# Sparse graph attention layer: roots of the second phase's layer norms by Newton steps on VectorE in place of ScalarE

## The reference

```python
def _ln(x, g, b):
    mu = jnp.mean(x, axis=-1, keepdims=True)
    var = jnp.var(x, axis=-1, keepdims=True)
    return (x - mu) * jax.lax.rsqrt(var + EPS) * g + b
...
z = _ln(x, ln1_g, ln1_b)
q, k, v = z @ Wq + bq, z @ Wk + bk, z @ Wv + bv       # per head
scores = jnp.einsum('ehd,ehd->eh', q[row], k[col]) * scale + bias
alpha = softmax of scores over the edges of each row
att = segment_sum(alpha * v[col], row) @ Wo + bo
x1 = x + att
z = _ln(x1, ln2_g, ln2_b)
ff = jax.nn.silu(z @ W1 + b1) @ W2 + b2
return _layernorm(x + (x1 + ff))
```

## Time and profile before

| | |
|---|---|
| median of 3 runs | 4988.64 us |
| lowest and highest run | 4966.76 and 5004.79 us |
| profiled execution: span | 4610.2 us |
| profiled execution: its own time | not given beside the span |
| TensorE busy, matmul | 3227.0 us (70%) |
| VectorE busy | 2862.0 us (62%), 6445 instructions |
| ScalarE busy | 2094.3 us (45%), 6748 instructions |
| GpSimd busy | 3100.7 us (67%), 3033 instructions |
| chain that ended last, by engine | issue 23%, PE 21%, POOL 16%, DVE 14%, DMA 11%, DVEq 9%, ACT 3% |
| mean granted TensorE clock | 0.794 |

### The profile page before, as it was taken

One profiled execution on the slowest core, in us unless ns is written; L12 is line 12 of the kernel. 1 busy time (PEld: TensorE's weight loads), 2 busy tenths in 40 slices (PEclk: granted clock), 3 DMA queues, 4 the chain that ended last, 5 costly groups with the idle time before them and its releaser, 6 DMA issues.

```text
span 4610.2 us, 73226 instructions
## 1 busy us (share of the span) xinstructions
PE 3227.0 (70%) x18717; PEld 2461.0 (53%) x18717; DVE 2862.0 (62%) x6445; ACT 2094.3 (45%) x6748; POOL 3100.7 (67%) x3033
## 2 busy tenths in 40 slices
PE   4576877776877546777677776777777777777766
PEld 3344444444444235666565665656656555656655
DVE  9766666666666335666556665666565565665654
ACT  0011112111111135666566666666566566665664
POOL 0177777777777767777777777777676676666752
PEclk5577766777767668888888888888888888888888
DMA  4233333333334355655666656665665665656542
GB/s 168 66 113 115 107 102 112 109 102 107 112 100 111 102 192 188 208 183 184 222 203 214 214 196 205 221 214 182 213 210 166 210 206 190 203 185 211 189 150 82
DMA packets 282999, 756.58 MB, mean 164 GB/s; under 512 B 92435, under 2 KB 94675, under 8 KB 281862
## 3 DMA queue, kind: packets, MB, share of 16 engines
q0 software_dynamic: 213664, 577.32, 38.1%
q1 hardware_dynamic: 68454, 169.70, 12.1%
HBM read 759.20 MB, written 58.87 MB: 177 GB/s over the span
## 4 chain that ended last, share of the span: by engine, by line
issue 23%; PE 21%; POOL 16%; DVE 14%; DMA 11%; DVEq 9%; ACT 3%; POOLq 1%; ACTq 1%; SPq 0%; PEld 0%; PEldq 0%
POOL records L378 8%; PE bank L1144 7%; DMA records<-rec_w,pos_i 5%; PE bank L1179 5%; POOL region_a L447 5%; DVE region_c L864 4%; PE bank L1227 3%; DMA region_a<-kv,cols 3%; DVEq L990 2%; DMA region_c<-hiT 2%; PE bank L1201 2%; DVEq L792 2%; DVE hi_oh L728 2%; ACT region_a L669 1%; PE bank L1093 1%
## 5 line engine op out<-in xcount | busy, mean ns | idle before, releaser
L447 POOL DMA_INDIRECT region_a<-kv,cols x1160 | 1311.3, 1130 | 449.5 <-issue 342.5
L378 POOL DMA_INDIRECT records<-rec_w,pos_i x1024 | 1046.9, 1022 | 534.3 <-issue 515.1
L669 ACT ACTIVATE region_a<-region_a,pr 128x64 f32<-128x64 f32 x4640 | 1132.5, 338 | 58.5 <-issue 46.6
L1179 PE MATMUL bank<-ident,region_a 128*128 128x128 f32 x4640 | 708.2, 308 | 345.5 <-issue 281.8
L864 DVE TENSOR_TENSOR region_c<-region_a,region_c 128x1024 f32<-128x1024 f32 x580 | 734.4, 1308 | 283.8 <-DMA region_a<-kv,cols 239.4
L1144 PE MATMUL bank<-ident,region_c 128*128 128x128 f32 x4640 | 664.9, 307 | 329.2 <-DVE region_c L864 329.0
L1179 PEld LDWEIGHTS bank<-ident,region_a 128*128 128x128 f32 x4640 | 619.1, 161 | 425.0 <-issue 322.6
L1144 PEld LDWEIGHTS bank<-ident,region_c 128*128 128x128 f32 x4640 | 624.1, 201 | 373.0 <-DVE region_c L864 372.9
L1093 PE MATMUL bank<-region_c 64*128 64x64 f32 x2048 | 346.4, 337 | 204.7 <-issue 178.9
L1093 PEld LDWEIGHTS bank<-region_c 64*128 64x128 f32 x2048 | 327.7, 248 | 293.4 <-issue 259.4
L542 ACT COPY rec_w<-region_a 128x64 f32 x128 | 31.3, 245 | 960.5 <-DMA records<-rec_w,pos_i 960.5
(11 more groups left out here) (147 smaller groups left out, 4264.8 us busy)
## 6 DMA issues: line engine op xcount, KB each, us to landing
region_c<-srcT SPq DMA_DIRECT2D x128, 512.0 KB
region_c<-hiT SPq DMA_DIRECT2D x128, 256.0 KB
region_a<-kv,cols POOLq DMA_INDIRECT x1160, 5.8
records<-rec_w,pos_i POOLq DMA_INDIRECT x1024
kv<-region_c SPq DMA_DIRECT2D x32, 512.0 KB
records<-pad_rec SPq DMA_DIRECT2D x16, 576.0 KB, 16.9
region_a<-in_x_dram SPq DMA_DIRECT2D x32, 256.0 KB
qx<-region_a SPq DMA_DIRECT2D x32, 256.0 KB
```

The lines of the kernel that those rows point to most:

```text
L378: pool.indirect_dma_start(records, bass.IndirectOffsetOnAxis(ap=pos_i[j % 2][:, s:s + 1], axis=0), rec_w[j % 2][:, s, :], None).then_inc(S ...
L447: pool.indirect_dma_start(KV[h][:, s, :], None, kv, bass.IndirectOffsetOnAxis(ap=cols[h][:, s:s + 1].bitcast(I32), axis=0), bounds_check=L ...
L669: last = act.activation(v, v, ACT.Copy, scale=pr[h][:, s, hd:hd + 1])
L1179: last = pe.matmul(vT_ps[:, c * P:(c + 1) * P], KV[h][:, s, C + c * P:C + (c + 1) * P], ident[:, :], start=s == 0 and c == 0, stop=s == GR ...
```

## The change

In the second phase ScalarE takes no root any more. `std_of` and `norms` are gone, with the semaphores `stats_end`, `stats_mid`, `std_end` and `std_mid`. VectorE has a new function, `inverse_root`: it guesses 1/sqrt(v) from the bits of v (one multiply and add on the word as an integer) and improves it in three Newton steps of two operations each, scaled so that the factors fold into one last multiplication. It is called in `last_norm` and `residual`, in the place of the reciprocal. ScalarE loads the exponent's table once, ahead of the second phase; the exponent, the tangent, the copy and the identity need no other, and no further load stands in the second phase of the built program. The first phase's norm keeps ScalarE's root.

```diff
+SEED = float(0x5F3759DF - (1 << 31))
...
+            act.preload_act_table(ACT.Exp)
             act.wait_ge(S["ng_out"], 16)
...
-            def std_of(stats_sem, std_sem, k):
-                act.wait_ge(stats_sem, k)
-                act.activation(std[:, :], mv[:, 1:2], ACT.Sqrt, bias=eps_t[:, :]).then_inc(std_sem, 1)
...
                     take_scT()
-                    norms(stage)
                     act.wait_ge(S["sc_ready"], g + 1)
...
-            def statistics(ps, stats_sem):
+            def statistics(ps):
                 dve.bn_stats(stats[:, :], ps)
                 dve.drain()
-                dve.bn_aggr(mv[:, :], stats[:, :]).then_inc(stats_sem, 1)
+                dve.bn_aggr(mv[:, :], stats[:, :])
+                dve.drain()
+
+            def inverse_root():
+
+                dve.tensor_scalar(var_w[:, :], mv[:, 1:2], EPS, None, ALU.add)
+                dve.drain()
+                dve.tensor_scalar(root[:, :].bitcast(I32), var_w[:, :].bitcast(I32), -0.5, SEED, ALU.mult, ALU.add)
+                for three in (3.0, 12.0, 768.0):
+                    dve.drain()
+                    dve.scalar_tensor_tensor(root_t[:, :], root[:, :], var_w[:, 0:1], root[:, :], ALU.mult, ALU.mult)
+                    dve.drain()
+                    dve.scalar_tensor_tensor(root[:, :], root_t[:, :], -three, root[:, :], ALU.add, ALU.mult)
+                dve.drain()
+                dve.tensor_scalar(rstd[:, :], root[:, :], 2.0 ** -13, None, ALU.mult)
+                dve.drain()
...
             def residual(k):
 
                 dve.tensor_tensor(s_w, z2, x_b2, ALU.add).then_inc(S["s_ready"], 1)
-                dve.wait_ge(S["std_mid"], k)
-                dve.reciprocal(rstd[:, :], std[:, :])
-                dve.drain()
+                inverse_root()
                 dve.tensor_scalar(z2, z2, mv[:, 0:1], rstd[:, 0:1], ALU.subtract, ALU.mult).then_inc(S["z2_ready"], 1)
...
             def last_norm(column):
-                dve.wait_ge(S["std_end"], dve.snap(n_out) + 1)
-                dve.reciprocal(rstd[:, :], std[:, :])
-                dve.drain()
+                inverse_root()
```

More of the change, by code:

```diff
@@ L185, in layer_kernel @@
         rstd = sb("rstd", [P, 1])
+        var_w = sb("var_w", [P, 1])
+        root = sb("root", [P, 1])
+        root_t = sb("root_t", [P, 1])
         perm = sb("perm", [P, NT + 2])
@@ L223, in layer_kernel @@
             att_sb wo_done z2_ready z2_turned z2_sb h_done0 h_done1 h_act0 h_act1 h_ready0 h_ready1 q_taken y_done out_ready out_sent consts_c
-            s_ready quiet restarted pool_held dve_held sp_held stats_end stats_mid std_end std_mid""".split()
+            s_ready quiet restarted pool_held dve_held sp_held""".split()
         S = {n: sem(n) for n in names}
@@ L572, in _ @@
             n_vT = act.alloc_register("act_vT")
-            n_end = act.alloc_register("act_end")
-            for r in (groups, n_scT, n_vT, n_end):
+            for r in (groups, n_scT, n_vT):
                 act.reg_mov(r, 0)
@@ L619, in _ @@
                 n = act.snap(count, min_val=1, max_val=NBLK)
-                def norms(stage):
-                    if stage == 1:
-                        with act.If(t > 1):
-                            act.reg_add(n_end, n_end, 1)
-                            std_of(S["stats_end"], S["std_end"], act.snap(n_end))
-                    if stage == 2:
-                        with act.If(t > 0):
-                            std_of(S["stats_mid"], S["std_mid"], t)
                 def tail(stage):
@@ L677, in _ @@
                 by_half(act, groups, lambda f: tile_groups(act, n, f, body, alone))
-            std_of(S["stats_end"], S["std_end"], NT - 1)
             take_vT()
             turn_att(NT)
-            std_of(S["stats_mid"], S["std_mid"], NT)
             turn_z2(NT)
@@ L684, in _ @@
                 hidden(NT, a)
-            std_of(S["stats_end"], S["std_end"], NT)
         @block.vector
@@ L898, in residual_stats @@
                 dve.drain()
-                statistics(z2, S["stats_mid"])
+                statistics(z2)
             def residual(k):
                 dve.tensor_tensor(s_w, z2, x_b2, ALU.add).then_inc(S["s_ready"], 1)
-                dve.wait_ge(S["std_mid"], k)
-                dve.reciprocal(rstd[:, :], std[:, :])
-                dve.drain()
+                inverse_root()
                 dve.tensor_scalar(z2, z2, mv[:, 0:1], rstd[:, 0:1], ALU.subtract, ALU.mult).then_inc(S["z2_ready"], 1)
@@ L918, in last_stats @@
                 dve.drain()
-                statistics(s_w, S["stats_end"])
+                statistics(s_w)
             def last_norm(column):
-                dve.wait_ge(S["std_end"], dve.snap(n_out) + 1)
-                dve.reciprocal(rstd[:, :], std[:, :])
-                dve.drain()
+                inverse_root()
                 hold(S["out_sent"], dve.snap(n_out) * 16)
```

## The result

Timed beside each other on one chip, the kernel before took 4977.7 us (median of 4 runs, 4934.98 to 5004.79) and the changed kernel 5079.95 us (4 runs, 5051.52 to 5088.23): a ratio of 1.0198 with a 95% interval of 1.0134 to 1.0263. The change costs some 100 us where 72 were forecast (a ratio of 1.0144). The profiled execution of the changed kernel took 5087.08 us, its span 5085.4 us.

The account below looks back on a forecast made before the run. VectorE, not ScalarE, was taken to be late. Four-group tiles 44, longer tiles 20, last two tiles 2.6 and the end 4.9 sum to 72 us slower: 4988.64 + 72 = 5060 us, range 4998 to 5108.

Parts of the forecast that it names:

- Price of the steps: VectorE, each of 64 norms: nine dependent operations 0.24 us apart replace one reciprocal, adding 1.9 us a norm (1.2 to 2.8).
- Stage 1's term: End norm's added 1.9 us lies between rescaling and values on VectorE, so TensorE's work behind comes 1.9 us later.
- -0.3 +1.9 -0.6: Stage 2, four-group tiles: 0.3 us back from the exponent's wait, 1.9 of steps before the next products, 0.6 from the collision.
- the collision: GpSimd's two additions slow VectorE's products behind s; 1.0 of 2.0 us given back in 9 four-group tiles, nothing in 6.
- the tail: Serial work behind the last tile, two end norms and one middle norm: together 4.9 us slower.
- the last two: Last two tiles, three groups each: only stage 1's 1.9 us counts, less some 0.6; 1.3 each, 2.6 us.
- the four-group term: Fifteen four-group tiles, no slack on VectorE at the tile's end: 2.9 us longer each, 44 us.
- the longer tiles: 14 longer tiles: waits for gathered rows hide stage 3's delay; late GpSimd gates leave 1.4 us a tile, 20 us.
- 378 us around the span, left as it is: Time by which the three-run median, 4988.64 us, exceeds the profiled span, 4610.2; taken as lying around it and unchanged.
- Absorbed: Rival: waits absorb most of the delay, only four-group tiles and the end count; 29 us slower, 5018 us; chance 0.24.
- Faster: Rival: ScalarE's own values start 0.86 us earlier and TensorE waits for those; gain 53 us, 4936 us; chance 0.07.
- Dearer: Rival: GpSimd's additions hold the steps up and all 64 norms cost 1.9 us in full; 5102 to 5120 us; chance 0.11.

Follow-up runs that it names:

- e3: Changed kernel with the nine root steps replaced by one reciprocal of the variance (output wrong, run for time): ratio 0.9977 to the kernel before.
- e2: Changed kernel with both norms' root steps moved behind the statistics, ahead of the stage's scores: ratio 1.0051 to the kernel before.
- e1: The kernel before, unchanged, run again on the fast chip for its trace: 4616.18 us, ratio 0.9998.
- e9: The kernel before, unchanged, run again on a slower chip (4982 us there) for its trace: ratio 1.0029.
- e5: The changed kernel, unaltered, run again on the slowest chip (kernel before 5028 us there): ratio 1.0225 to the kernel before.
- e10: The changed kernel, unaltered, on the chip where the kernel before took 4982 us: 5083.04 us, ratio 1.0193 to the kernel before.
- e11: Changed kernel with s written after the middle norm's steps, on the chip where the kernel before took 4982 us: ratio 1.0168 to the kernel before.
- e7: Changed kernel with the end norm's steps moved to stage 1's gap, the middle norm's left in place; slowest chip: ratio 1.0207 to the kernel before.
- e6: Changed kernel with the middle norm's steps moved to stage 2's gap, the end norm's left in place; slowest chip: ratio 1.0106 to the kernel before.
- e8: Changed kernel with both norms' roots done together in stage 2's gap (13 operations), last_norm moved there; slowest chip: 4990.93 us, ratio 0.9935 to the kernel before.
- e12: Changed kernel with the nine root steps done twice in each norm: 5235.66 us, ratio 1.0503 to the kernel before.
- e4: Changed kernel with s written after the middle norm's steps, on the fast chip: 4702.42 us, ratio 1.0179 to the kernel before.

## Why the prediction was right, and where it was not

The forecast was a ratio of 1.0144, the measurement 1.0198. The direction and the mechanism held, the size was too small by some 30 us, and the largest term of the sum was the one that was off.

**What is late.** VectorE, not ScalarE, was the engine that the tile waits for: e3 bears it out with 10.6 us for 352 us of ScalarE's time, and e2 with 1.0051 for the same steps in another place. The step that ScalarE's work up to the exponent gets shorter and hardly anything waits for it held.

**Price of the steps.** 0.24 us apart was taken; the timeline has 0.23 to 0.29 (the form with a scalar read from memory is the 0.29), and 2.2 to 2.3 us for nine. Stage 1's term, 1.9, measured 5.56 - 3.61 = 1.95.

**Stage 2.** The term "-0.3 +1.9 -0.6" was mis-sized twice. The first part: the 0.3 was read from the fast chip's trace, where VectorE waits for the exponent 31 times (9.5 us in e1); on e9's chip it does so 3 times, 1.1 us in all, so there was nothing to get back. The values came 0.33 later behind the scores instead (2.48 against 2.15), with an idle time of 0.44 us that the trace puts to nothing it knows. It is there in e5, e10, e11 and in e7, and not in e6, e8 or e12 (2.11, 2.11, 2.12); the cause stays open. The second part was that 1.0 of the collision's 2.0 us is given back in 9 tiles and nothing in the other 6. Already the first profile has products of 5.7 us or more behind s in 14 of the 15 tiles, and e9 has 6.6 in all 15, so the 11 waits of the earlier trace rows were too few to count them by. With the change all of the collision moved out of the products, in every tile, and all of it came back in the steps. The give-back is 1.98 on one side and, on the other, 4.21 where 1.9 of steps were added. So nothing came back net: the stretch from the values to stage 3's scores is 2.06 longer, where the sum had 1.9 - 0.6 = 1.3, with or without the collision in the steps (e11).

**The four-group tile.** 2.9 was forecast; 4.55 is what the changed kernel's first trace shows against e9 (90.56 less 86.01) and 5.39 what e10's does. The terms above explain 1.95 + 0.33 + 2.06 = 4.3. What is left is spread over stretches the change does not touch (by the first trace and by e10's: from the tile's first products to its scores +0.23 and +0.64, from the hidden layer to the next tile +0.58 and +0.88, from stage 1's values to stage 2's scores -0.45 and -0.31). This last one is where the fast chip swallowed stage 1's delay in e4 (-2.10). The forecast took its waits from a trace of the fast chip and let the delay through, which fits the slower chips, on which the result was measured; that it fits them is luck, since no row of the slower kind had been read. e4, close to the change, costs 81 us there (4702.42 less 4621.33); by its trace and e1's it is 2.5 us for each four-group tile, 2.5 for each of the 11 five-group ones and 11 in the tail. TensorE, in order and waiting longer at L1143 and L1172, shows a lower granted clock in these tiles: from 3700 to 4700 us, in stretches of 200, 0.85 to 0.88 of 2.4 GHz in e9, 0.80 to 0.84 in the changed kernel's first trace and 0.79 to 0.85 in e10's, means of time at its two levels of 1.2 and 2.4 GHz. e9 above, the changed kernel below (the granted clock is the third number from the end):

```profile
4500.00:4700.00 200.00, 141.51 (x928) 119.05 (x926) 115.73 (x204) 127.67 (x423) 129.24 (x129) 0.88 0.56 183
```

```profile
4500.00:4700.00 200.00, 130.91 (x789) 109.94 (x788) 112.96 (x221) 85.52 (x330) 120.70 (x123) 0.80 0.58 192
```

That this is what lengthens them is argued and not shown; e12, which waits most, has the shortest stretch from the hidden layer to the next tile (13.00 against e9's 13.84).

**The rest of the sum.** By the changed kernel's first trace and e9's: four-group tiles 15 x 4.55 = 68 (forecast 44); the 11 tiles with five groups 1.63 each, 18, and the first four tiles 2 (together 20, forecast 20); the tail 5.5 (forecast 4.9); the last two nothing (2.6). 68 + 18 + 2 + 5.5 = 94, and the spans differ by 5085.4 - 4993.7 = 92. So the step that failed is the four-group term, by 24 us, and nothing else of size in this pair of traces. e10's trace puts more on the long tiles (2.47 each) and on the first four (12), but its profiled execution was the longest of its four, 5127.1 against a median of 5083.04. The match of 20 with 20 for the longer tiles is therefore in part luck. e10's four-group tile, 5.39 longer, is also above what I expected of it (2.9 to 3.9).

**The level.** "378 us around the span, left as it is" was harmless for the difference, but the reading was wrong: 2 us lie around it (e1), and the rest was another chip. The range's upper end was called the middle of the dearer case, 5102 to 5120; that middle is 5111, not 5108. The lower end, 4998, has no working.

**The rivals.** Absorbed: half of it is seen in the longer tiles, where about 1.6 of 3.5 us comes through (2.5 by e10's trace), but not as a whole. On the fast chip e4 shows the four-group tiles absorbing stage 1's delay, which this rival had not said. Faster: ruled out by e3, 2 to 20 us where 53 were needed; TensorE waits for VectorE. Dearer: its mechanism is there, its price is not. The steps are held by GpSimd, as the rival said, one of 0.22 us for 3.07; the Trainium skill ("SBUF — State Buffer", "SBUF: two separate sides") has the loser wait for the whole instruction of the other. The row agrees in kind and goes further: the step is held until two additions of 1.27 us each are over. (Which of GpSimd's instructions held it from 4565.20 to 4565.76, before the additions began, the trace doesn't tell.) But e4 and e11 take the collision away from the steps, and the stretch it lies in stays the same (17.01 against 17.02): the rival counted the loss and not the equal gain in the products. The times of e10 and e11 alone wouldn't settle it. Nor do all norms count in full: e12's second set does, 2.4 us for each of 64, the first does not.

**Both norms.** e5 costs 111 us, and e6, with only the end norm late, 54; so the middle norm's place costs 57. e7's 97 us are not the middle norm's alone: its end norm pays the same 2.2 us of a tile ahead of stage 1's scores (17.71 against e5's 15.49) that it saves behind them (3.29 against 5.57). e7's expectation counted 0.95 us of it as hidden, a wait read from the fast chip. A run with only the middle norm late and the end norm truly hidden wasn't made.

## What to carry to other kernels

Taking 352 us off an engine that nobody waits for gave 0.2%, and putting 2 us a norm into the queue of the engine that everybody waits for cost ten times that. So look, before work is moved between engines, at what is waited for behind its new place, and put it where the receiving engine waits anyway: the same steps cost 2% in front of the values and 0.5% in the gaps (on the fast chip), and with both norms in one gap the kernel gained 0.65% (on the slowest). Look also at how long the gap is: stage 1's hid 0.95 us of 2.5 on the fast chip and nothing on the slowest. And read the waits from a trace of the kind of chip on which the times are taken. A chain of small dependent steps is paid by its number, so two norms side by side take 2.8 us instead of 4.4.

## What the runs showed of the hardware

- One kernel on different chips: 4621, 4982 and 5028 us (medians of 25, 13 and 11 runs). The first phase differs most: the second starts at 1649 us in e1 and 1927 us in e9. GpSimd's indirect writes of the records in it are as long in both (the last column is idle time and what ended it), but on the slower chip they wait for VectorE's indices, e1 first, then e9:

```profile
L378 POOL DMA_INDIRECT records<-rec_w,pos_i x1024 | 1048.0, 1023 | 536.3 <-issue 517.4 <-DVE pos_i L806 14.6 <-ACT rec_w L545 4.3
```

```profile
L378 POOL DMA_INDIRECT records<-rec_w,pos_i x1024 | 1045.5, 1021 | 816.6 <-issue 513.5 <-DVE pos_i L806 297.2 <-ACT rec_w L545 5.9
```

- A VectorE step on one element a partition costs 0.23 to 0.24 us from start to start with constants, and 0.29 where its scalar is read from memory; a second one that doesn't depend on it costs 0.13 more (two L859 in 0.35 us).
- VectorE can sit idle with its input ready. On the fast chip it reads stage 2's scores 0.04 us after TensorE's fold ends (e1, e4), on the slower ones 2.2 us after it in e9 and 3.9 in e5 (means of 15 four-group tiles); the trace names "remote" for most of these waits, and the cause is open.
- A step of 0.22 us can be held for 3.07 us by GpSimd's operations, while GpSimd's additions beside it take 1.27 us each, not 1.57 and 2.24: the collision changes hands, its sum stays.
